# LN3's rstd in PSUM, a doubled scratch and a first group by halves in a Mamba block with a mixture of experts

## The reference

```
h = concat(patches(x) @ W + b, txt) + pos                 # 64 x 114 x 256
xz = layernorm(h) @ W_in;  xi, z = split(xz)              # 512 channels each
xc = silu(causal_conv4(xi));  dt, B, C = split(xc @ W_x)  # 16 states
delta = softplus(dt @ W_dt + b_dt);  u = delta * xc
s_t = exp(delta_t * A) * s_(t-1) + u_t * B_t;  y = sum_n(s * C) + xc * D
h = h + (y * silu(z)) @ W_out                             # LN2 follows
v = silu(x @ sw1 + b1) * (x @ sw2 + b2)
h = h + layernorm(v) @ sw3 + b3                           # layernorm(v) is LN3
rows picked by an index also get a softmax-weighted top-1 of 8 experts
```

## Time and profile before

| what | value |
|---|---|
| median of 3 runs | 1761.15 us (1760.6 to 1761.76) |
| the profiled execution | 1761.73 us, span 1759.5 us |
| mean granted TensorE clock | 0.946 of full speed |
| busy: VectorE, GpSimd | 1581.9 us, 1569.3 us |
| busy: TensorE, ScalarE | 1483.8 us, 1333.5 us |
| DMA | 217.98 MB, 124 GB/s over the span |

### The profile page before, as it was taken

One profiled execution on the slowest core, in us unless ns is written; L12 is line 12 of the kernel. 1 busy time (PEld: TensorE's weight loads), 2 busy tenths in 40 slices (PEclk: granted clock), 3 DMA queues, 4 the chain that ended last, 5 costly groups with the idle time before them and its releaser, 6 DMA issues.

```text
span 1759.5 us, 27824 instructions
## 1 busy us (share of the span) xinstructions
PE 1483.8 (84%) x9824; PEld 1066.7 (61%) x9824; DVE 1581.9 (90%) x1387; ACT 1333.5 (76%) x3100; POOL 1569.3 (89%) x782
## 2 busy tenths in 40 slices
PE   7778888888898888888988888889888888887588
PEld 6655666655666666556666665666666655654355
DVE  2499999999999999999999999999999999998935
ACT  2577788788787888888878888888788888886644
POOL 0699999999999999999999999999999999998804
PEclk9888999999999999999999999999999999996799
DMA  3767755555666655556666555566665555656110
GB/s 110 153 129 187 153 133 119 119 128 127 143 127 142 135 117 123 125 127 143 126 143 139 116 124 120 127 144 126 142 140 117 125 117 131 138 120 134 35 34 15
DMA packets 194140, 217.98 MB, mean 124 GB/s; under 512 B 93979, under 2 KB 184485, under 8 KB 193490
## 3 DMA queue, kind: packets, MB, share of 16 engines
q1 hardware_dynamic: 193234, 215.04, 55.6%
q0 software_dynamic: 576, 1.17, 0.3%
q10 hardware_dynamic: 192, 0.01, 0.0%
HBM read 169.92 MB, written 46.62 MB: 123 GB/s over the span
## 4 chain that ended last, share of the span: by engine, by line
DVE 42%; ACT 17%; issue 15%; PE 14%; POOL 10%; DMA 1%; SPq 1%; DVEq 0%; ACTq 0%; POOLq 0%
DVE psum L1292 19%; DVE xr L1292 15%; POOL xr L1618 6%; ACT psum L995 6%; DVE xr L1301 3%; PE psum L607 3%; POOL xr L1626 3%; DVE vv L1363 2%; ACT L1117 2%; ACT L1026 2%; PE psum L694 2%; PE psum L779 2%; ACT soft L1047 2%; ACT soft L1051 2%; ACT soft L1043 2%
## 5 line engine op out<-in xcount | busy, mean ns | idle before, releaser
L1618 POOL TENSOR_TENSOR xr<-u,bbc 128x912 f32<-128x912 f32 x512 | 1079.3, 2139 | 14.9 <-DMA u<-u_scratch 14.9
L995 ACT ACTIVATE psum<-delta,a_neg 128x228 f32<-128x228 f32 x2048 | 805.9, 440 | 221.8 <-DVE xr L1301 192.0
L1292 DVE TENSOR_TENSOR_SCAN psum<-psum,xr 128x912 f32<-128x912 f32 x320 | 656.1, 2050 | 68.0 <-ACT psum L995 57.3
L1626 POOL TENSOR_TENSOR xr<-xr,cbc 128x912 f32<-128x912 f32 x192 | 409.0, 2130 | 33.8 <-DVE xr L1292 30.9
L1292 DVE TENSOR_TENSOR_SCAN xr<-psum,xr 128x912 f32<-128x912 f32 x192 | 392.3, 2043 | 0.0
L1301 DVE TENSOR_TENSOR xr<-psum,cbc 128x912 f32<-128x912 f32 x320 | 353.6, 1105 | 11.1
L708 PE MATMUL psum<-xr,fold 128*32 128x228 f32 x4096 | 295.7, 386 | 54.8 <-POOL xr L1626 27.9
L607 PE MATMUL psum<-xh,win 128*128 128x228 f32 x1024 | 226.0, 371 | 62.5 <-ACT xs L1026 33.0
L607 PEld LDWEIGHTS psum<-xh,win 128*128 128x128 f32 x1024 | 194.7, 195 | 93.7 <-ACT xs L1026 43.7
L658 PE MATMUL psum<-xi,conv_d 128*128 128x228 f32 x1024 | 210.9, 358 | 0.0
L708 PEld LDWEIGHTS psum<-xr,fold 128*32 128x32 f32 x4096 | 96.9, 112 | 183.4 <-issue 80.8
(11 more groups left out here) (201 smaller groups left out, 1602.1 us busy)
## 6 DMA issues: line engine op xcount, KB each, us to landing
delta<-delta_scratch SPq DMA_DIRECT2D x256, 228.0 KB, 6.5
u<-u_scratch SPq DMA_DIRECT2D x256, 228.0 KB, 4.2
bbc<-bc_scratch SPq DMA_DIRECT2D x128, 114.0 KB, 2.6
u_scratch<-u SPq DMA_DIRECT2D x64, 228.0 KB, 5.1
cbc<-bc_scratch SPq DMA_DIRECT2D x128, 114.0 KB, 2.7
delta_scratch<-delta SPq DMA_DIRECT2D x64, 226.0 KB, 5.8
out<-ob SPq DMA_DIRECT2D x32, 228.0 KB
h_scratch<-h SPq DMA_DIRECT2D x31, 228.0 KB
```

What stands on the lines that cost most here:

```text
L995: ins = nc.scalar.activation(slot(k)[:, j * TOK:(j + 1) * TOK], delta4[:, c // 2, j, c % 2], ACT.Exp, scale=a_neg[:, c, j, n:n + 1])
L1292: nc.vector.tensor_tensor_scan(x if k in ON_POOL else slot(k), slot(k), x, 0.0, ALU.mult, ALU.add).then_inc(scan_done, 1)
L1618: nc.gpsimd.tensor_tensor(xr[:, k % XRING], u4[:, c // 2, :, c % 2], bbc[:, p, n].unsqueeze(1).to_broadcast([P, J, TOK]), ALU.mult).then_i ...
L1626: nc.gpsimd.tensor_tensor(xr[:, k % XRING], xr[:, k % XRING], cbc[:, p, k % NI].unsqueeze(1).to_broadcast([P, J, TOK]), ALU.mult).then_inc ...
```

## The change

In words, in the order of the program:
- Opening, TensorE: 12, 4 and 6 products of the constant `mean_w` with itself, written to a bank that nobody reads before it is overwritten, stand before the first tokens, before the first variance and before the first projection.
- Opening, VectorE, GpSimd, SP: group 0's delta is formed in two halves (`first_delta`), ahead of the image tokens of group 1; u's first half is VectorE's, its second GpSimd's. SP stores and spreads the first half before it turns to the second.
- `u_scratch` and `delta_scratch` exist twice, for even and odd groups. `delta_out` and `u_out` wait for the stores of the group before, the stores for the reads of two groups before.
- Loop: `ln3_rstd` writes its result to `vvar_ps` in PSUM and `v_norm` reads it there; `ffn_sigmoid` waits for `v_done` instead of `vn_done`.
- GpSimd's constants for the experts move from the tail to step 6; the products of their bias (`bias_rows`) from TensorE's tail to step 31, unit 13, and VectorE's sum with them to step 32.
- Tail: `turn_rows(0)` before `ffn_out(ga)`, `hidden(0, 0)` before `v_var(gz)`, VectorE's `expert_stats(0)` before `v_norm(ga)`.

```
 bc_scratch = nc.dram_tensor("bc_scratch", (2, 2 * NS, TOK), F32, kind="Internal").ap()
-u_scratch = nc.dram_tensor("u_scratch", (2, J, DQ, 2 * TOK), F32, kind="Internal").ap()
-delta_scratch = nc.dram_tensor("delta_scratch", (2, J, DQ, 2 * TOK), F32, kind="Internal").ap()
+u_scratch = nc.dram_tensor("u_scratch", (2, 2, J, DQ, 2 * TOK), F32, kind="Internal").ap()
+delta_scratch = nc.dram_tensor("delta_scratch", (2, 2, J, DQ, 2 * TOK), F32, kind="Internal").ap()
 h2_scratch = nc.dram_tensor("h2_scratch", (ROWS, DM), F32, kind="Internal").ap()
...
-    def keep_u(half):
-        rows = u_scratch[half].rearrange("j d x -> (j d) x")
+    def keep_u(g, half):
+        need(sp, u_in[half], 16 * NQ * (g - 1))
+        rows = u_scratch[g % 2, half].rearrange("j d x -> (j d) x")
         sp.dma_start(rows, u[:, 2 * half:2 * half + 2].rearrange("p c t -> p (c t)")).then_inc(u_out_s[half], 16)
-    def delta_rows(half):
-        return delta_scratch[half].rearrange("j d (z t) -> (j d) z t", t=T)
-    def keep_delta(half):
-        sp.dma_start(delta_rows(half)[:, :, 1:],
+    def keep_delta(g, half):
+        need(sp, delta_in[half], 16 * NQ * (g - 1))
+        rows = delta_scratch[g % 2, half].rearrange("j d (z t) -> (j d) z t", t=T)
+        sp.dma_start(rows[:, :, 1:],
                      delta[:, 2 * half:2 * half + 2].rearrange("p c (s t) -> p (c s) t", s=SEQ)[:, :, 1:]
...
-    def spread(scratch, dst, half, done):
-        rows = scratch[half].rearrange("j d x -> d j x")
+    def spread(rows, dst, half, done):
         for q in range(NQ):
             sp.dma_start(dst[q * DQ:(q + 1) * DQ, half].rearrange("p j c t -> p j (c t)"),
-                         rows).then_inc(done[half], 16)
-    def spread_half(g, half):
+                         rows.rearrange("j d x -> d j x")).then_inc(done[half], 16)
+    def half_free(g, half):
...
         need(sp, exp_done, UNITS * (g - 1) + UNITS // 2 * (half + 1))
+    def spread_u(g, half):
         sp.wait_ge(u_out_s[half], 16 * (g + 1))
-        spread(u_scratch, u4, half, u_in)
-        sp.wait_ge(delta_out_s[half], 16 * (g + 2))
-        spread(delta_scratch, delta4, half, delta_in)
+        spread(u_scratch[g % 2, half], u4, half, u_in)
+    def spread_delta(g, half):
+        sp.wait_ge(delta_out_s[half], 16 * (g + 3))
+        spread(delta_scratch[g % 2, half], delta4, half, delta_in)
+    def spread_half(g, half):
+        half_free(g, half)
+        spread_u(g, half)
+        spread_delta(g, half)
...
             sp.wait_ge(delta_done, 1 + half)
-            keep_delta(half)
-        for half in range(2):
+            keep_delta(0, half)
             sp.wait_ge(u_done, 1 + half)
-            keep_u(half)
-        for half in range(2):
-            spread_tensor(0, half, delta_scratch, delta4, delta_out_s, 32, delta_in)
-            spread_tensor(0, half, u_scratch, u4, u_out_s, 16, u_in)
+            keep_u(0, half)
+            spread_delta(0, half)
+            spread_u(0, half)
             if half == 0:
...
                 sp.wait_ge(delta_done, 2 * i + 3 + half)
-                keep_delta(half)
+                keep_delta(i + 1, half)
             for half in range(2):
                 sp.wait_ge(u_done, 2 * i + 3 + half)
-                keep_u(half)
+                keep_u(i + 1, half)
             spread_half(i + 1, 0)
...
     sp.wait_ge(const_pool, CONST_POOL)
-    for half in range(2):
-        sp.dma_start(delta_scratch[half].rearrange("j d x -> (j d) x"),
-                     delta[:, 2 * half:2 * half + 2].rearrange("p c t -> p (c t)")).then_inc(delta_out_s[half], 16)
+    for a in range(2):
+        for half in range(2):
+            sp.dma_start(delta_scratch[a, half].rearrange("j d x -> (j d) x"),
+                         delta[:, 2 * half:2 * half + 2].rearrange("p c t -> p (c t)")).then_inc(delta_out_s[half], 16)
     def experts():
...
+    def bias_rows():
+        pe.wait_ge(ew_in, EW_IN)
+        pe.wait_ge(pool_c, 4)
+        pe.wait_ge(sz_done, 2 * GROUPS)
+        for x in range(E):
+            mm = pe.matmul(psum[0:E, CB, 0:DM], selb_e[:, x], e3[:, x], start=(x == 0), stop=(x == E - 1))
+        mm.then_inc(eb3_mm, 1)
     def before_first():
...
         for k in range(UNITS):
+            if i == GROUPS - 1 and k == 13:
+                bias_rows()
             if runs(i):
...
+    def idle_turns(n):
+        for _ in range(n):
+            pe.matmul(psum[:, YB, 0:P], mean_w[:], mean_w[:], start=True, stop=True)
     def first():
+        pe.wait_ge(const_pool, CONST_POOL)
+        idle_turns(12)
         pe.wait_ge(token_in, TOKEN_IN)
...
         center(0)
+        idle_turns(4)
         var(0)
+        idle_turns(6)
         pe.wait_ge(conv_in, CONV_IN)
...
     pe.wait_ge(gw_in, GW_IN)
-    pe.wait_ge(ew_in, EW_IN)
     v_center(ga)
...
     v_var(ga)
-    bias_rows()
     ffn_in(gz)
+    turn_rows(0)
     ffn_out(ga)
-    turn_rows(0)
     v_center(gz)
     turn_rows(1)
+    hidden(0, 0)
     v_var(gz)
-    hidden(0, 0)
     turn_rows(2)
...
         if g < GROUPS - 2:
-            need(act, vn_done, g)
+            need(act, v_done, g)
         else:
...
         act.wait_ge(lv3_done, g + 1)
-        nc.scalar.activation(gate_of(g), vsq[:], ACT.Exp, scale=-0.5).then_inc(rs3_done, 1)
+        nc.scalar.activation(vvar_ps(g), vsq[:], ACT.Exp, scale=-0.5).then_inc(rs3_done, 1)
...
+    def first_delta(half):
+        lo, hi = 2 * half, 2 * half + 2
+        dve.wait_ge(spl_done, 1)
+        dve.wait_ge(delta_out_s[half], 32)
+        nc.vector.scalar_tensor_tensor(out=delta[:, lo:hi], in0=dt_bank(half), scalar=0.0, in1=soft[:, lo:hi],
+                                       op0=ALU.max, op1=ALU.add).then_inc(delta_done, 1)
+        if half == 0:
+            dve.wait_ge(delta_done, 1)
+            dve.wait_ge(xs_done, 2)
+            nc.vector.tensor_tensor(u[:, lo:hi], delta[:, lo:hi], xs[:, 0, lo:hi], ALU.mult).then_inc(u_done, 1)
     def delta_out(g):
...
         for half in range(2):
-            need(dve, delta_in[half], 16 * NQ * g)
+            dve.wait_ge(delta_out_s[half], 16 * (g + 2))
         nc.vector.scalar_tensor_tensor(out=in_banks(delta), in0=dt_banks, scalar=0.0, in1=in_banks(soft),
...
         dve.wait_ge(rs3_done, g + 1)
-        nc.vector.tensor_tensor(vv_of(g), vv_of(g), gate_of(g), ALU.mult).then_inc(vn_done, 1)
+        nc.vector.tensor_tensor(vv_of(g), vv_of(g), vvar_ps(g), ALU.mult).then_inc(vn_done, 1)
     def before_first():
+        for half in range(2):
+            first_delta(half)
         image_tokens(1)
-        delta_out(0)
         means_out()
...
         ln2_stats(GROUPS - 1)
+        dve.wait_ge(eb_in, EB_IN)
+        dve.wait_ge(eb3_mm, 1)
+        nc.vector.tensor_tensor(eb3x, psum[0:E, CB, 0:DM], eb3r, ALU.add).then_inc(eb3_done, 1)
         ffn_gate(GROUPS - 2)
...
         for half in range(2):
-            dve.wait_ge(delta_out_s[half], 16)
+            dve.wait_ge(delta_out_s[half], 32)
...
     ln2_moments(gz)
+    expert_stats(0)
     v_norm(ga)
-    expert_stats(0)
     expert_stats(1)
...
     expert_rows(1)
-    dve.wait_ge(eb_in, EB_IN)
-    dve.wait_ge(eb3_mm, 1)
-    nc.vector.tensor_tensor(eb3x, psum[0:E, CB, 0:DM], eb3r, ALU.add).then_inc(eb3_done, 1)
     expert_stats(3)
...
         pool.wait_ge(delta_done, 2 * g + 2)
+        if g == 0:
+            pool.wait_ge(u_done, 1)
+            nc.gpsimd.tensor_tensor(u[:, 2:], delta[:, 2:], xs[:, p, 2:], ALU.mult).then_inc(u_done, 1)
+            return
         for half in range(2):
-            need(pool, u_in[half], 16 * NQ * g)
+            need(pool, u_out_s[half], 16 * g)
         nc.gpsimd.tensor_tensor(u[:], delta[:], xs[:, p], ALU.mult).then_inc(u_done, 2)
+    def expert_constants():
+        nc.gpsimd.memset(half_neg[:], -0.5).then_inc(pool_c, 1)
+        nc.gpsimd.iota(prio_i[:], [[-1, E]], base=E, channel_multiplier=0).then_inc(pool_c, 1)
+        nc.gpsimd.memset(selb_e[:], 0.0).then_inc(pool_c, 1)
+        pool.wait_ge(pool_c, 3)
+        pool.wait_ge(gw_in, GW_IN)
+        nc.gpsimd.tensor_copy(selb_e[:].rearrange("p a b -> p (a b)")[:, 0:E * E:E + 1],
+                              selb[:].to_broadcast([P, E])).then_inc(pool_c, 1)
+        nc.gpsimd.tensor_copy(prio[:], prio_i[:]).then_inc(pool_c, 1)
...
         q = 1 - p
+        if i == 6:
+            expert_constants()
         for k in range(UNITS):
...
```

More of the change, by code:

```diff
@@ L489, in rows_out @@
                                          rows.partition_broadcast(DQ)).then_inc(done, 16)
-                    def spread_tensor(g, half, scratch, dst, stored, count, done):
-                        need(sp, dbu_done, UNITS * (g - 1) + UNITS // 2 * (half + 1))
-                        need(sp, exp_done, UNITS * (g - 1) + UNITS // 2 * (half + 1))
-                        sp.wait_ge(stored[half], count)
-                        spread(scratch, dst, half, done)
                     def before_first():
@@ L916, in turn_hot @@
                         mm.then_inc(hot_mm, 1)
```

(13 more changed lines are left out.)

## The result

| | before | changed |
|---|---|---|
| median | 1761.45 us (1760.6 to 1762.02, 4 runs) | 1729.22 us (1728.01 to 1730.28, 4 runs) |
| the profiled execution, its span | 1761.73, 1759.5 us | 1728.77, 1726.7 us |
| mean granted TensorE clock | 0.946 | 0.947 |

The ratio is 0.9816, interval 0.9803 to 0.9828: 32 us less. The forecast was 1724 with a range of 1715 to 1738, so the time is inside it, and 5 us of the gain of 37.9 are missing. Three marks on VectorE divide both spans: its whole-group delta in step 0, and `gate` of group 30 at the end of step 31.

The account below looks back on a forecast made before the run. VectorE was taken to bound the loop, at 50.19 us a step with GpSimd close behind. 1761.73 - 27.6 (rstd in PSUM) - 7.5 (opening) - 2.8 (end) = 1723.8, forecast 1724 us, range 1715 to 1738.

Parts of the forecast that it names:

- rstd in PSUM: Loop: v_norm's wait for GpSimd's product goes, 1.32 to 0.37 us in 29 calls, 27.6 us saved.
- bound at the dear end: Loop: v_norm at 0.455 us a call, like L1358's product with PSUM operand and pointers, saving 25.1 us.
- Doubled scratch: Loop: neither old wait of delta_out and u_out is the late one, so nothing gained or lost.
- Opening: Before the loop: unread products 4.0 us plus halves 3.5 us, 7.5 us saved, ends 0.2 and 9.8.
- The clock's part: Opening, TensorE: unread products raise the clock for tokens, mean, centring and projection; 4.0 us taken, between -2.2 and 4.5.
- The halves: Opening: group 0's first delta half 2.4 us sooner, transfers start earlier, fewer SP waits; 3.5 us saved, 2.4 to 5.3.
- the 3.72 us of stall: Opening: VectorE's stall behind TensorE's wait for group 2's patches, which can shrink by at most 3.72 us.
- End: After the loop: ffn_out chain 2.3 us sooner, bias rows moved 0.5 us; 2.8 us saved, ends -4 and +4.6.
- Rival 2: Opening gives almost nothing: clock stays low with tokens 2.2 us late, or second delta half late; 1731 us, chance 12%.
- Rivals 1, 3 and 4: 1: GpSimd paces or wait moves, 1738 us, 6%; 3: v_norm stays long, 1751, 4%; 4: TensorE's clock falls, 1799, 2%.

Follow-up runs that it names:

- product to PSUM: Changed kernel with v_norm reading two SBUF operands again and writing its product to PSUM: 1757.35 us, ratio 0.9973 to the kernel before.
- rstd in PSUM alone: Kernel before with one edit, LN3's rstd written to PSUM and read there by v_norm: 1737.2 us, ratio 0.9858 to before.
- Group 0 whole: Changed kernel with group 0's delta and u whole, in the old order, unread products kept: 1725.26 us, again 1729.24; ratios 0.9788 and 0.9807 to before.
- without the unread products: Changed kernel without the 22 unread TensorE products at the start: 1733.94 us, ratio 0.9835 to the kernel before.
- patches ahead: Changed kernel with group 2's patches loaded ahead of the second half's stores and reads on SyncE: 1720.41 us, ratio 0.9759 to before.

## Why the forecast was nearly right

The loop carries it: 27.6 us forecast and measured. Outside the loop 10.3 us were forecast and 5.2 came.

**rstd in PSUM: right in mechanism and size.** Forecast 0.37 us a call, step 49.24, 27.6 us in all; measured 0.382, 49.26 and 27.6. That the sum agrees to the tenth is in part chance: 27 full steps gave 0.925 each, and the rest came from the last step and what follows it. The wait before u_out was put at 0.2 and is 0.34, since I had not counted that GpSimd's product is held up as well. My bound at the dear end, 0.455, was not needed. As to the Trainium skill, "VectorE: DVE Perf Modes", section on the TRN2 errata, by which the prediction's estimate was 0.46: the trace does not agree; in the tail the same operation took 0.396 with SBUF operands and 0.39 with one in PSUM. The Trainium skill, "SBUF — State Buffer", "Who interferes with whom", says that two SBUF inputs exclude GpSimd and one does not: by product to PSUM and rstd in PSUM alone, the runs agree.

**Doubled scratch: right,** nothing either way.

**Opening: the step that failed is the second.** The clock's part was put at 4.0 with 4.5 as the end where it is up in time; softplus ended 5.2 us sooner, a little over that end. The halves were put at 3.5 (2.4 to 5.3), on the sentence that "halves in sequence save part of SP's waits for landings". They add to them: 12.3 us of standing queue for 3.6 before. Group 0 whole puts their worth at nothing that can be told, and without the unread products the opening with them is 2.3 us longer than before. Of the 5.2 us that the clock gave, 3.3 arrived at the end of the opening, and that is the better end of what was seen: five profiled executions of this opening lie at 86.49 to 87.75, two of the old one at 89.83 and 88.29. The stall before the image tokens, which was to go to under 1 us, went to 6.09; that sign was missed. I had taken the patches of group 2 as the end of a train limited by its bytes. Limited it was (share 1.08 for 27 us before); but the train now has two gaps of 5.5 us together, and the patches need not be its end: the run with the patches ahead shows that they can go in front of the second half, with their buffer free since TensorE's last use at 34.6. The 3.72 us of stall that I called reachable were reachable, by one moved line, and the kernel with it gains 9.1 us in the opening (89.83 - 80.77), near the upper end of 9.8 that I gave, where the change gained 3.3.

**End: right in sign, 1.9 for 2.8 in the profiled execution.** ffn_in came 3.6 us closer to h2_turn (forecast 3.5). Of that, 1.7 were lost because the last products of group 30 ahead of it ran at the lower level (1.14, 1.06, 1.06, 1.03 us, where they took 0.6 to 0.7), and what was left ended at the hidden product, as forecast. The bias rows were priced between 2.3 won and 4 lost, 0.5 taken; slow they cost 2.14 and bring 2.4 back, 0.2 won, fast they bring the end to 84.8. One sign of being wrong, the last reduces later behind the bias rows, so came true in this execution and not in the other.

**Rivals.** Rival 2, the opening nearly empty, was half true, though for neither of its two reasons. Rivals 1, 3 and 4 did not occur: no new wait in the loop, v_norm short, and the loop's steps even but for the last, which has its wait of 2.9 us as before.

## What to carry to other kernels

In a queue that works in order, price a step by what the queue waits for as well as by the bytes: here, cutting a store-then-read in halves doubled the landings it stood still for, and the transfers ran dry meanwhile. A load whose buffer is free belongs ahead of such a wait. Where VectorE and GpSimd are both near the bound, look for short instructions with two SBUF inputs whose mean is some times that of their like in a quiet stretch, and put one input in PSUM. A TensorE chain with gaps has two prices; with products that nobody reads in the gap just ahead of it, it had the lower one in three profiled executions of three.
